# The input projection as three f32r products of high and low parts, with x loaded in four transfers

## The reference

```python
xt = jnp.transpose(x, (0, 2, 1))
q = xt @ Wq.T                                # 1024 x 512 times 512 x 512, per batch
qh = q.reshape(B, T, NH, dk).transpose(0, 2, 1, 3)      # 8 heads of 64
scores = scale * jnp.einsum('bhqd,bhkd->bhqk', qh, qh)
logits = (scores * cmask + (1.0 - cmask) * NEG) * rmask
attn = jax.nn.softmax(logits, axis=-1)
ctx = jnp.einsum('bhqk,bhkd->bhqd', attn, qh)
out = ctx.transpose(0, 2, 1, 3).reshape(B, T, D) @ Wo.T
x = x + jnp.transpose(out, (0, 2, 1))
x = x + conv1d(x, cond_2048) + L1_cond_b     # the second layer
```

## Time and profile before

| what | value |
|---|---|
| median of 3 runs | 4175.13 us (4171.65 to 4175.92) |
| the profiled execution's own time | 4174.45 us |
| its span, first to last instruction | 4172.7 us |
| TensorE busy | 4055.7 us (97%) |
| ScalarE busy | 2709.2 us (65%) |
| GpSimd busy | 2543.2 us (61%) |
| VectorE busy | 2417.5 us (58%) |
| mean granted TensorE clock | 0.992 of full speed |

### The profile page before, as it was taken

The page is one execution under the profiler, slowest core; times in us unless marked ns, Lnnn a source line. Parts: engine busy times, 40 slices in busy tenths (PEclk is TensorE's granted clock), DMA queues, the critical chain, the costliest instruction groups (busy, mean ns, idle before and its releaser), DMA issues. The chain is left out here.

```text
span 4172.7 us, 57357 instructions
## 1 busy us (share of the span) xinstructions
PE 4055.7 (97%) x18688; PEld 2506.5 (60%) x18688; DVE 2417.5 (58%) x2260; ACT 2709.2 (65%) x3782; POOL 2543.2 (61%) x1042
## 2 busy tenths in 40 slices
PE   7999999999999999999999999999999999999799
PEld 4665656566565655655565665556556555655598
DVE  4664555556565655656565565656556465656676
ACT  4775757667575766757576675757667575766465
POOL 4775767667575766757576675757667575766200
PEclk8999999999999999999999999999999999999999
DMA  4433434343343434344343434434433443443588
GB/s 111 106 87 91 104 94 114 91 105 92 91 105 88 117 92 101 92 94 104 86 117 92 101 92 93 108 83 117 97 97 92 97 106 81 116 97 76 147 292 265
DMA packets 308543, 451.95 MB, mean 108 GB/s; under 512 B 155043, under 2 KB 223267, under 8 KB 308134
## 3 DMA queue, kind: packets, MB, share of 16 engines
q1 hardware_dynamic: 308262, 448.18, 42.5%
HBM read 112.28 MB, written 67.11 MB: 43 GB/s over the span
## 5 line engine op out<-in xcount | busy, mean ns | idle before, releaser
L725 POOL TENSOR_TENSOR plo<-p,phi 128x1024 fp32r<-128x1024 f32 x1024 | 2539.3, 2491 | 1349.0 <-ACT phi L656 1344.1
L654 ACT ACTIVATE p<-sc 128x512 f32<-128x512 f32 x2048 | 1108.9, 594 | 815.9 <-PE sc L527 676.1
L769 DVE TENSOR_REDUCE mrow<-misc 128x1 f32<-128x1024 f32 x1024 | 1203.0, 1216 | 731.2 <-PE misc L488 731.1
L656 ACT ACTIVATE phi<-p 128x1024 fp32r<-128x1024 f32 x1024 | 1086.1, 1061 | 32.5
L526 PE MATMUL sc<-quer,keys 128*128 128x512 f32 x2048 | 912.1, 445 | 22.9 <-issue 13.1
L539 PE MATMUL pv<-phi,val 128*96 128x512 f32 x2048 | 857.5, 419 | 18.3 <-issue 18.3
L527 PE MATMUL sc<-quer,keys 96*128 96x512 f32 x2048 | 810.8, 396 | 0.0
L541 PE MATMUL pv<-phi,val 128*64 128x512 f32 x2048 | 806.4, 394 | 0.0
L545 PE MATMUL pv<-plo,val 128*96 128x512 f32 x2048 | 639.0, 393 | 0.9 <-POOL plo L725 0.9
L539 PEld LDWEIGHTS pv<-phi,val 128*96 128x96 f32 x2048 | 330.1, 161 | 339.7 <-issue 184.6
L526 PEld LDWEIGHTS sc<-quer,keys 128*128 128x128 f32 x2048 | 387.7, 189 | 192.5 <-issue 69.0
(11 more groups left out here) (70 smaller groups left out, 2823.7 us busy)
## 6 DMA issues: line engine op xcount, KB each, us to landing
keys<-hi SPq DMA_DIRECT2D x256, 256.0 KB, 3.2
quer<-mhi SPq DMA_DIRECT2D x256, 256.0 KB, 5.0
keys<-lo SPq DMA_DIRECT2D x128, 256.0 KB, 5.7
quer<-mlo SPq DMA_DIRECT2D x128, 256.0 KB, 3.8
xo<-x SPq DMA_DIRECT2D x64, 512.0 KB, 4.8
x<-xo SPq DMA_DIRECT2D x64, 512.0 KB, 4.9
xin<-x SPq DMA_DIRECT2D x16, 2048.0 KB, 13.4
out<-stage SPq DMA_DIRECT2D x64, 512.0 KB, 6.4
```

Of the source, the lines that this page charges most:

```text
L654: act.activation(p32[:, t % NP32, half(h)], sc[:, h, :], ACT.Exp, scale=SCALE).then_inc(s_p32, 1)
L656: act.activation(phi[:, t % NPHI, :], p32[:, t % NP32, :], ACT.Copy).then_inc(s_phi, 1)
L725: pool.tensor_tensor(plo[:, t % NPLO, :], p32[:, t % NP32, :], phi[:, t % NPHI, :].bitcast(F32), ALU.subtract).then_inc(s_plo, 1)
L769: reduced = dve.tensor_reduce(mrow[:, q:q + 1], misc[:, k, :], AX.X, ALU.max)
```

## The change

The projection's weights and x are each split into a high f32r part (a rounding copy on ScalarE) and a low part (the difference). TensorE multiplies high by high, low weights by high x, and high weights by low x: twelve f32r matmuls a half where there were four f32 ones. The product of the two low parts is left out.

The weights and the first batch's x are split in `start()`. The x of every later batch arrives in four transfers of 512 KB in head (2,0), between the moves of the operands. ScalarE rounds the four parts in head (2,1) at t = 0, 2, 3 and 4. GpSimd subtracts parts 0 and 2 (after its split of t = 0 and 3), VectorE parts 1 and 3 (at t = 2 and 6). The low part overwrites the loaded x (`x32` and `xl` are one place). The unsplit weights borrow the place of `ct`, and several tiles are laid elsewhere in memory to make room.

```diff
@@ SyncE
-                if staged is not None:
-                    sp.wait_ge(s_masked, staged)
-                sp.dma_start(xb[:], x_v[b]).then_inc(s_x, 16)
+            def load_x(b, k):
+                sp.dma_start(x32[:, k, :], x_v[b][:, k, :]).then_inc(s_xk[k], 16)
+
+            def load_mask(b, staged):
+                sp.wait_ge(s_masked, staged)
                 sp.dma_start(mask[:], cond_v[b].to_broadcast([P, T])).then_inc(s_x, 16)
...
                 for i in range(2):
                     move(keys[0:DK, k + i, :], hi, i).then_inc(s_kq[i], 16)
+                if then is not None:
+                    load_x(then, 0)
                 sp.wait_ge(s_mhi, pair(b, p) + 1)
...
+                if then is not None:
+                    load_x(then, 1)
                 sp.wait_ge(s_lo, pair(b, p) + 1)
...
+                        if phase != "last" and (p, i) == (2, 0):
+                            load_x(b + 1, 2)
...
                             rows(nb, np_, ni)
+                        if phase != "last" and (p, i) == (2, 0):
+                            load_x(b + 1, 3)
@@ TensorE, project
-                    pe.wait_ge(s_x, 32 * nb + 32)
-                for k in range(DT):
-                    last = pe.matmul(out, wq[:, k, np_ * P:(np_ + 1) * P], xb[:, k, half(h)],
-                                     start=(k == 0), stop=(k == DT - 1))
+                    pe.wait_ge(s_xl, split_done(nb, 2, 2))
+                    pe.wait_ge(s_xl_pool, 2 * nb)
+                cols = slice(np_ * P, (np_ + 1) * P)
+                for n, (w, xs) in enumerate(((wqh, xh), (wql, xh), (wqh, xl))):
+                    for k in range(DT):
+                        last = pe.matmul(out, w[:, k, cols], xs[:, k, half(h)],
+                                         start=(n == 0 and k == 0), stop=(n == 2 and k == DT - 1))
@@ ScalarE
+HI_AT = {0: 0, 2: 1, 3: 2, 4: 3}
+            def input_high(b, k):
+                act.wait_ge(s_xk[k], 16 * b)
+                act.activation(xh[:, k, :], x32[:, k, :], ACT.Copy).then_inc(s_xh, 1)
...
+                act.activation(wqh[:, :, 0:P], wq32[:, :, 0:P], ACT.Copy).then_inc(s_wqh, 1)
+                act.activation(xh[:, :, half(0)], x32[:, :, half(0)], ACT.Copy).then_inc(s_xh, 1)
...
                             exponentials(b, p, i, t, first)
+                            if phase != "last" and (p, i) == (2, 1) and t in HI_AT:
+                                input_high(b + 1, HI_AT[t])
@@ GpSimd
+LO_POOL = {0: 0, 3: 2}
+            def input_low(b, k):
+                pool.wait_ge(s_xh, split_done(b, DT, k + 1))
+                pool.tensor_tensor(xl[:, k, :], x32[:, k, :], xh[:, k, :].bitcast(F32), ALU.subtract).then_inc(s_xl_pool, 1)
...
                             split(b, p, i, t, phase == "first" and p == 0 and i == 0)
+                            if phase != "last" and (p, i) == (2, 1) and t in LO_POOL:
+                                input_low(b + 1, LO_POOL[t])
@@ VectorE
+LO_DVE = {2: [1], 6: [3]}
+                weights_low(0, slice(0, P))
+                first_low(0)
+                first_low(1)
...
+                weights_low(1, slice(P, D))
...
+                            if phase != "last" and (p, i) == (2, 1):
+                                for k in LO_DVE.get(t, []):
+                                    input_low(b + 1, k)
```

More of the change, by code:

```diff
@@ L189, in build_attention, with sb @@
     with ExitStack() as ctx:
-        def sb(name, shape, dt):
-            return ctx.enter_context(nc.sbuf_tensor(name, shape, dt))
+        def sb(name, shape, dt, where=ctx):
+            return where.enter_context(nc.sbuf_tensor(name, shape, dt))
         def ps(name, shape):
@@ L197, in sem @@
             return ctx.enter_context(nc.semaphore(name))
-        wq = sb("wq", [P, DT, D], F32)
+        wqh = sb("wqh", [P, DT, D], F32R)
+        wql = sb("wql", [P, DT, D], F32R)
         wo = sb("wo", [P, PAIRS, D], F32)
@@ L202, in build_attention @@
         ident = ident_r[:].bitcast(F32)
-        xb = sb("xb", [P, DT, T], F32)
+        xh = sb("xh", [P, DT, T], F32R)
+        with ExitStack() as place:
+            x32 = sb("x32", [P, DT, T], F32, place)
+        xl = sb("xl", [P, DT, T], F32R)
         mask = sb("mask", [P, T], F32)
@@ L234, in build_attention @@
         s_x = sem("s_x")
+        s_x0 = sem("s_x0")
+        s_xk = [sem(f"s_xk{k}") for k in range(DT)]
+        s_wq = sem("s_wq")
+        s_wqh = sem("s_wqh")
+        s_wql = sem("s_wql")
+        s_xh = sem("s_xh")
+        s_xl_pool = sem("s_xl_pool")
+        s_xl = sem("s_xl")
         s_mask8 = sem("s_mask8")
@@ L317, in tok, with split_done @@
             return slice(t * P, (t + 1) * P)
+        def split_done(b, per, of):
+            return 2 + per * (b - 1) + of
         x_v = x.rearrange("b (k p) t -> b p k t", p=P)
@@ L338, in move, with operands @@
                 return sp.dma_start(dst.bitcast(F32), part[DK * i:DK * i + DK, :].bitcast(F32))
-            def operands(b, p):
+            def operands(b, p, then=None):
                 k = 2 * (p % 2)
@@ L421, in batch @@
                         if phase != "last" and (p, i) == (2, 1):
-                            load_x(b + 1, pair(b, 3) + 1)
+                            load_mask(b + 1, pair(b, 3) + 1)
                         if i == 0 and not end:
-                            operands(*next_pair(b, p))
+                            operands(*next_pair(b, p), b + 1 if phase != "last" and p == 2 else None)
+                        if phase != "last" and (p, i) == (2, 0):
+                            load_x(b + 1, 2)
                         if phase != "first" and (p, i) == (1, 0):
@@ L663, in do @@
                         values(phase, b, step, item, nxt)
+            def input_high(b, k):
+                act.wait_ge(s_xk[k], 16 * b)
+                act.activation(xh[:, k, :], x32[:, k, :], ACT.Copy).then_inc(s_xh, 1)
             def start():
+                act.wait_ge(s_begin, 32)
+                act.activation(wqh[:, :, 0:P], wq32[:, :, 0:P], ACT.Copy).then_inc(s_wqh, 1)
+                act.activation(xh[:, :, half(0)], x32[:, :, half(0)], ACT.Copy).then_inc(s_xh, 1)
+                act.wait_ge(s_x0, 16)
+                act.activation(xh[:, :, half(1)], x32[:, :, half(1)], ACT.Copy).then_inc(s_xh, 1)
                 do("start", 0, 0, "pair", PHASES["start"]["pair"], None)
+                act.wait_ge(s_wq, 16)
+                act.activation(wqh[:, :, P:D], wq32[:, :, P:D], ACT.Copy).then_inc(s_wqh, 1)
                 do("start", 0, 0, "head", PHASES["start"]["head"], (0, 0, 0))
@@ L830, in do, with weights_low, first_low, input_low @@
                         residual(phase, b, step, item, b - 1, item[1] + 1)
+            def weights_low(part, cols):
+                dve.wait_ge(s_wqh, part + 1)
+                dve.tensor_tensor(wql[:, :, cols], wq32[:, :, cols], wqh[:, :, cols].bitcast(F32), ALU.subtract).then_inc(s_wql, 1)
+            def first_low(h):
+                dve.wait_ge(s_xh, h + 1)
+                dve.tensor_tensor(xl[:, :, half(h)], x32[:, :, half(h)], xh[:, :, half(h)].bitcast(F32), ALU.subtract).then_inc(s_xl, 1)
+            def input_low(b, k):
+                dve.wait_ge(s_xh, split_done(b, DT, k + 1))
+                dve.tensor_tensor(xl[:, k, :], x32[:, k, :], xh[:, k, :].bitcast(F32), ALU.subtract).then_inc(s_xl, 1)
             def start():
```

30 lines of the change are left out of this document (18 added, 12 removed).

## The result

| | before | after |
|---|---|---|
| median of the runs | 4174.38 us (4171.65 to 4175.92) | 4222.34 us (4220.88 to 4226.7) |
| ratio, 95% interval | 1 | 1.0117 (1.01 to 1.0135) |
| span of the profiled execution | 4172.7 us | 4225.0 us |
| mean granted clock | 0.992 | 0.979 |

What follows compares the result with a forecast made beforehand. The prediction took TensorE, busy 97% of the span, to bound the kernel. From 4174.5 us it took 77 for the projection, added 36 for the splits and 3.5 for the start, and said 4138, range 4102 to 4164.

Steps and rivals of the forecast that it cites:

- What bounds the kernel: TensorE, busy 97%: projection savings come off the whole; work put on other engines in head (2,1) may come on top.
- The projection: On TensorE, twelve f32r matmuls at 235 ns save 0.61 us a half, 77 us over 126 halves.
- the one with 216 ns: Rival: f32r matmuls run faster in the projection than in the scores, 216 ns each, giving 4109 us; chance 0.10.
- The start: Before the loop, splitting weights and x makes the first projection 3.5 us late, bounds 2 and 5.
- The transfers: In head (2,0), two x quarters ahead of `keys<-lo` delay it about 4.2 us at most; 4.4 us slack, no cost.
- The x transfers hold up the operands: Rival: x parts delay `keys<-lo`, TensorE stands still 3.5 us a batch in head (2,1), 4190 us; chance 0.05.
- The clock drops in head (2,1): Rival: TensorE's waits in steps 4 to 7 bring 1.2 GHz, 1.7 us a batch, 4164 us; chance 0.12.
- 2.5 us a batch: Operand delay at which the late-operands rival decides: 37 / 15, with `keys<-lo` landing at 2127.
- The splits: In head (2,1), GpSimd and ScalarE work exceeds the head's time: 2.4 us before each of 15 batches, 36 us.
- the 28 that the prediction named as a sign of being wrong: The forecast is wrong if head (2,1) takes over 28 us; it expected 25 to 26.
- The splits stay hidden: Rival: ScalarE and GpSimd idle time in head (2,1) absorbs the splits, giving 4102 us; chance 0.12.
- The sum: Whole kernel: 4174.5 - 77 + 36 + 3.5 = 4137.0, 4137.7 on the median's footing, said as 4138 us.

Runs made afterwards that it cites:

- experiment 10: Changed kernel with all x parts issued behind the row, both engines' early subtractions and three reciprocals moved, low-part wait only ahead of the third product: 4098.69 us.
- 4: Kernel before, f32 projection and no splits, with x loaded in four parts at the changed kernel's four places: 4246.3 us, ratio 1.0172.
- experiment 7: experiment 5 with a 0.07 us memset of 16 columns right ahead of VectorE's subtraction: 4156.54 us, ratio 0.9962.
- Experiment 1: Changed kernel with each of the four loop transfers of x cut to 4 of 1024 columns, splits reading a resident weight tile: 4126.87 us, ratio 0.9883.
- experiment 2: Changed kernel with its four transfers but without the roundings and subtractions of x in the loop: 4168.81 us, ratio 0.9988.
- experiment 5: Changed kernel with all four parts of x issued in head (2,0) behind the row quer<-mneg: 4128.61 us, ratio 0.9887.
- 8: Changed kernel with only the third part of x moved behind the row quer<-mneg: 4194.09 us, ratio 1.006.
- Experiment 6: Changed kernel with twelve more f32r matmuls, results overwritten, ahead of the wait for the row in head (2,1) step 0: 4188.9 us, ratio 1.0038.
- experiment 3: Changed kernel with the four transfers cut to 4 columns and no roundings or subtractions in the loop: 4091.24 us, ratio 0.9805.

## Why the prediction was wrong, point by point

**What bounds the kernel: right.** Outside pair 2 nearly all that the projection saved came off the whole, as the next figure shows. In head (2,1) the waits decided.

**The projection: right, 0.61 a half forecast, 0.65 measured.** 60.9 us over 94 halves of the other pairs. In the rows above twelve matmuls took 2.74 us, 228 ns between starts, where the sum went by 235. Of the rivals, the one with 216 ns falls.

**The start: right, at the upper end of what was measured.** 3.5 forecast, 3.6 measured. The other experiments up to 10, but for 4, have the same start, and in their profiles it took 48.37 to 50.00 us, so 2.0 to 3.6 more than before. In experiment 7 the projection's matmuls are at full rate from 14.85, in the changed kernel from 18.21: when the clock came up made most of the difference. VectorE's two subtractions took 4.49 us together (2.4 forecast for one), and the first matmul waits for it until 11.61, where the prediction had 12.0:

```profile
11.61 2.05 PE L511 MATMUL misc<-xh,wqh 128*128 128x512 f32 x4 [11.61 <-DVE xl L899]
```

**The transfers: the step that failed.** The prediction said: "The 4.4 us of slack hold them, and this costs nothing." That was worked out for `keys<-lo` alone. For the third and fourth part it asked only when they themselves were needed, in steps 3 and 4 of (2,1). It never asked what stood behind the third in the queue. There stands a row of 4 KB, `quer<-mneg`, which is made late in head (2,0) and needed at the first scores of (2,1), a few microseconds later. Before, it was so quick that it had no wait outside the start, and so no row in the waits to draw the eye. Experiments 1, 2, 4, 5 and 8 show the cause from both sides: it appears with the transfers alone, in the old kernel too, goes with their bytes or with their place, and shrinks by 1.0 us for 512 KB. It costs 5.07 us a batch (experiment 2), 76 us in all: 3.35 of waiting and 1.70 behind it, which goes with the lower clock. Experiment 6 has about as much of the clock, 1.9, in the changed kernel.

The bytes themselves did not break the slack that the prediction had worked out: `keys<-lo` landed at 2397.73 and 2398.89 in the head above, and the maxima of step 0, which need the first of the two, came at 2402.38 and did not wait for it.

**The rivals on this point.** "The x transfers hold up the operands" had the mechanism, the sign and nearly the price of the wait (3.5 us against 3.2), but for `keys<-lo`, whose slack held as said, and without the clock's part. At 0.05 it was held far too unlikely, since the evidence against it was about another transfer. "The clock drops in head (2,1)" was right that TensorE's new waits bring the 1.2 GHz, as behind the gap of the earlier trace rows, and right about steps 4 to 7 in ten of fifteen batches. It missed step 0, where the longer gap is. No rival took both. The prediction named 2.5 us a batch as the point from which the change is slower, and the row's lateness alone was above it.

**The splits: the size right, the way right only once the row was out of it.** 2.4 us a batch forecast, 2.25 measured in experiment 5, by the chain that was forecast (ScalarE's exponentials behind GpSimd): head (2,1) takes 25.36 us there, where the forecast had 25 to 26. In the changed kernel it takes 28.54, above the 28 that the prediction named as a sign of being wrong. In the changed kernel itself they cost 8.67 - 5.07 = 3.6, along another way: TensorE's late start shifts the engines against each other, VectorE's subtraction takes 2.67 instead of the 1.22 with a wait that was assumed, and TensorE waits 1.8 us a batch, not 0.7, for the maxima. About as much again is the clock's: it is at half for 7.05 us of a pair 2 instead of the 3.87 with the transfers alone, and at half clock half of the time is lost, an estimate of 1.6 us. "The splits stay hidden" is false as the change stands and almost true of experiment 10, which puts them elsewhere.

**The sum with what was measured.** Without transfers and splits, pair 2 should be 53.25 - 2 x 0.65 = 51.95; experiment 3 has 51.91. The whole is 4174.5 - 126 x 0.65 + 3.6 + 15 x 8.67 = 4226.2, against 4226.7 of the profiled execution. Most of these terms come from the same traces, so this says that nothing is left over, and is no test of its own. Without the failed step, with the splits at 2.25: 4129.9, against 4128.6 of experiment 5. So the forecast's 4138 was within 10 us of a kernel with the four issues a few lines further down.

## What to carry to other kernels

When a transfer is put at a new place, list everything that is issued behind it on its queue, the tiny ones too, with the time at which each is needed. A small transfer without a wait in the profile is one whose slack nobody has measured. Where TensorE is the bound, reckon a new gap of about 3 us at one and a half times its length (5.07 us for 3.35 in experiment 2), and don't put a VectorE instruction that reads two SBUF tiles ahead of something a PSUM bank waits for while GpSimd is busy.

## What the runs showed of the hardware that was not expected

- VectorE and GpSimd, both reading two tiles in SBUF, take turns, and whose turn it is can hang on 0.07 us: the same subtraction took 1.23 us (experiment 5, GpSimd's beside it 3.44), 2.67 (after), or 3.52 (7, behind the memset, GpSimd's beside it 2.42). Experiment 1, 27 us longer in one of five executions, with 3.55 in that one, suggests that one kernel can fall either way; its other executions have no profile, so this is not shown.
- A row of 4 KB behind three parts of 512 KB came 7.9 us after its issue (2392.53 to 2400.38), while the DMA engines together moved 243 to 287 GB/s.
- At the 2.8 us gap the clock fell to 1.2 GHz and stood there for 6.8 us, while the gap of 1.67 us at the loop's edge mostly left it at 2.4 GHz. It is not one gap, one fall: with the transfers alone (experiment 2) two of the fifteen gaps, 3.0 and 2.8 us from start to start, have none. Filling the gap with matmuls that nobody needs gave 33 us back.
- f32r matmuls of 128x512 followed each other in 228 ns in the projection, a little less than the 235 of the scores.
